# One store of the whole output after the last stage, in place of sixteen stores inside it

## The reference

```python
x = x + attention(layernorm(x))          # 16 heads of 32, causal
x = x + experts(layernorm(x))            # 32 experts, top 8, width 192
x = x + state_space(layernorm(x))        # scan in chunks of 64, inner width 1024
x = x + _L1_ffn_ref(layernorm(x), lut, gate_idx, up_idx, down_idx)

def _L1_ffn_ref(x, lut, gate_idx, up_idx, down_idx):
    gate = _ghost_linear(x, gate_idx, lut)   # x @ lut[gate_idx].T, 512 -> 1376
    up = _ghost_linear(x, up_idx, lut)
    h = jax.nn.silu(gate) * up
    return _ghost_linear(h, down_idx, lut)   # 1376 -> 512
return x
```

## Time and profile before

| | us |
|---|---|
| median of 3 runs | 2704.81 |
| the three runs | 2699.21, 2706.01, 2704.81 |
| the profiled execution, its own time | 2699.21 |
| span of the profile (first to last instruction) | 2697.7 |
| outside the span (2699.21 - 2697.7) | 1.5 |
| TensorE busy in the span | 2395.8 (89%) |
| mean granted clock of TensorE | 0.934 of full speed |

### The profile page before, as it was taken

One profiled execution on the slowest core, in us unless ns is written; L12 is line 12 of the kernel. 1 busy time (PEld: TensorE's weight loads), 2 busy tenths in 40 slices (PEclk: granted clock), 3 DMA queues, 4 the chain that ended last, 5 costly groups with the idle time before them and its releaser, 6 DMA issues. The chain is left out here.

```text
span 2697.7 us, 48584 instructions
## 1 busy us (share of the span) xinstructions
PE 2395.8 (89%) x12839; PEld 1818.7 (67%) x12840; DVE 1580.2 (59%) x3443; ACT 964.2 (36%) x2184; POOL 976.6 (36%) x878
## 2 busy tenths in 40 slices
PE   7969999994756999999999759999979898799998
PEld 5855555552545888888888638888855554688886
DVE  6246566662664455555555466999278786555554
ACT  3114555552153444444444322222255453222221
POOL 3138888885003566666666301111111110000000
PEclk9978999997866999999999979999989999799999
DMA  5469999995345899999988544447499550100001
GB/s 175 124 198 316 346 338 354 335 332 140 84 156 159 243 265 275 236 255 259 275 234 210 89 138 140 172 164 226 136 237 201 132 150 9 40 24 23 23 9 63
DMA packets 263501, 491.18 MB, mean 182 GB/s; under 512 B 32081, under 2 KB 149329, under 8 KB 253650
## 3 DMA queue, kind: packets, MB, share of 16 engines
q1 hardware_dynamic: 197394, 272.17, 33.7%
q0 software_dynamic: 62976, 212.42, 27.9%
q10 hardware_dynamic: 3024, 5.29, 0.6%
HBM read 592.96 MB, written 198.79 MB: 293 GB/s over the span
## 5 line engine op out<-in xcount | busy, mean ns | idle before, releaser
L1367 PE MATMUL m_ps_u<-m_ring,m_xT_hi 128*128 x1280 | 373.0, 353 | 36.7 <-DMA m_ring<-w_split 34.1
L1333 POOL DMA_INDIRECT expert_sum<-x_res,token_of x160 | 254.0, 1587 | 230.1 <-ACT x_res L1435 134.8
L1367 PEld LDWEIGHTS m_ps_u<-m_ring,m_xT_hi 128*128 128x128 f32 x1280 | 238.4, 191 | 40.8 <-issue 40.6
L779 ACT ACTIVATE probs<-ps_c 128x512 f32<-128x512 f32 (+3 forms) x384 | 182.2, 490 | 213.3 <-PE ps_c L712 132.6
L809 DVE TENSOR_REDUCE neg_max<-ps_r 128x1 f32<-128x512 f32 (+3 forms) x256 | 147.6, 589 | 159.3 <-PE ps_r L679 109.6
L1490 DVE SCALAR_TENSOR_TENSOR m_h<-m_silu,m_xg,m_ps_u 128x128 f32<-128x128 f32 x160 | 55.6, 348 | 278.0 <-ACT m_silu L1429 278.0
L1367 PE MATMUL m_ps_u<-m_ring,m_xT_lo 128*128 x640 | 218.3, 341 | 0.0
L1326 POOL DMA_INDIRECT m_xg<-x_rows,token_of x160 | 176.7, 1105 | 103.8 <-issue 99.2
L679 PE MATMUL ps_r<-k_st,q_st 96*128 96x512 f32 (+3 forms) x384 | 163.3, 432 | 46.3 <-DVEq L802 18.2
L1803 PE MATMUL s_ps<-s_x_lo,s_w_hi 128*128 128x512 f32 x512 | 201.2, 393 | 0.0
L1803 PE MATMUL s_ps<-s_x_hi,s_w_lo 128*128 128x512 f32 x512 | 201.0, 393 | 0.0
(11 more groups left out here) (337 smaller groups left out, 5754.4 us busy)
## 6 DMA issues: line engine op xcount, KB each, us to landing
m_ring<-w_split SPq DMA_DIRECT2D x160, 1536.0 KB
m_ring<-w_split SPq DMA_DIRECT2D x160, 768.0 KB
w_split<-e_gu_parts POOLq DMA_DIRECT2D x32, 1536.0 KB
proj<-s_out SPq DMA_DIRECT2D x32, 1024.0 KB, 4.0
e_raw_gu<-w_experts POOLq DMA_DIRECT2D x32, 768.0 KB
w_split<-e_dn_parts POOLq DMA_DIRECT2D x32, 768.0 KB
e_raw_dn<-w_experts POOLq DMA_DIRECT2D x32, 512.0 KB
q_st<-q_parts SPq DMA_DIRECT2D x32, 256.0 KB, 6.3
```

Of the source, the lines that this page charges most:

```text
L779: nc.scalar.activation(probs[a][j % RING][:, :width], ps_c[a][:, :width], ACT.Exp, scale=SCALE).then_inc(exp_done, 1)
L1333: pool.indirect_dma_start(acc[j % 2], rows_at(j), y[j % TURNS], None, bounds_check=PADDED - 1, oob_is_err=True, compute_op=ALU.add).then_i ...
L1367: last = nc.tensor.matmul(ps_u[b % 2][:, :W_UP], x[b % 2][:, k, :], ring[:, first + k * GU_ROW:][:, bass.ds(place, W_UP)], start=(n == 0), ...
```

## The change

The sixteen waits and stores and the final wait leave SP's list in `lut_feed_forward`, which no longer takes `out`. A new function `store_tokens` runs after it, in a block of its own: SP issues one DMA of the whole of `x_res`, 4096 KB, and waits for it. The order of rows in DRAM is the same: each piece is a row of 512 values, 2 KB.

```diff
+def store_tokens(nc, x_res, out):
+    with ExitStack() as ctx:
+        stored = ctx.enter_context(nc.semaphore("out_stored"))
+        block = ctx.enter_context(nc.Block())
+
+        @block.sync
+        def _(sp):
+            sp.dma_start(out.rearrange("(n p) d -> p n d", p=P), x_res[:, :, :]).then_inc(stored, 16)
+            sp.wait_ge(stored, 16)
 
-def lut_feed_forward(nc, x_res, ident, w_ffn, out):
+def lut_feed_forward(nc, x_res, ident, w_ffn):
...
-        stored = sem("out_stored")
...
             load(2 * BODIES, 0, LAST_ROWS)
-            out_rows = out.rearrange("(n p) d -> p n d", p=P)
-            for i in range(TILES):
-                sp.wait_ge(added, SUB + BODIES * RUNS * SUB + i + 1)
-                sp.dma_start(out_rows[:, i, :], x_res[:, i, :]).then_inc(stored, 16)
-            sp.wait_ge(stored, 16 * TILES)
...
-        lut_feed_forward(nc, x_res, ident, w_ffn, out)
+        lut_feed_forward(nc, x_res, ident, w_ffn)
+        store_tokens(nc, x_res, out)
```

## The result

| | before | after |
|---|---|---|
| median of this comparison, us (6 runs each) | 2701.5 | 2722.24 |
| range, us | 2694.64 to 2706.01 | 2717.35 to 2724.44 |
| span of the profiled execution, us | 2697.7 | 2722.9 |
| ratio, with 95% interval | | 1.0067 [1.0048, 1.0086] |

The change makes the kernel slower, by 18 us by this ratio (0.0067 x 2701.5). The ratio is estimated from the executions of one comparison and is not the quotient of the two medians, which lie 20.7 us apart. Three more executions of the changed kernel, outside the six of the table, took 2711.59, 2715.37 and, profiled, 2724.37 us. The forecast was the right way, +10.4 us, but the median of 2722.2 lies above the forecast's range, which ended at 2720. The question is where 18 us come from when one late transfer was priced at 10.4.

What follows compares the result with a forecast made beforehand. Bound by TensorE almost without a gap, then VectorE's last additions and the last store's landing. Terms: -2.2 (last landing) + 0.3 (boundary) + 12.4 (new landing) = +10.4 on 2704.8, giving 2715.2 us; range 2708.4 to 2720.

Steps and rivals of the forecast that it cites:

- Removed stores cost nothing: Last stage: SP's sixteen waits and issues, 0.33 us each, are covered; only the last store's 2.2 us landing is saved.
- rival 3: Last run: store traffic slows matmuls and clock, removal gives 3.2 us back, +7.2 us, within 0.3%; chance 0.03.
- The boundary: Between last stage and new store: ending one block and starting another costs 0.27 us, upper bound 1.03.
- Rival 2: Kernel end: store lands after 13.1 us and block hand-over costs 1.03 us, +11.9 us, 2716.7; chance 0.15.
- The landing: Kernel end: the lone 4096 KB store lands 12.4 us after issue, bounds 11.1 and 13.1.
- twin: In `route`: an existing 4096 KB copy of the same tile in 2 KB pieces, landing after 13.1 us, used as model.
- rival 1: Kernel end: the late store runs at 437 GB/s and lands after 11.1 us, +9.2 us, 2714.0; chance 0.10.
- The deduction of 0.7 us from the twin: In `route`: 272 KB issued ahead on the same queue take 0.7 us of the copy's 13.1, leaving 12.4.
- Rival 4: Last stage: each of sixteen small stores holds up the path 2.2 us; one large store saves 22.5 us, 2682.3; chance 0.01.
- the scatter: Whole executions: three runs before spread from 5.6 us below their median to 1.2 above; two more us added on top.
- as before, at about 2695: End of last stage: sign that the last additions would end at about 2695 us of the span, unmoved.
- a shift of this kind: Whole program: a shift between two programs' medians, unrelated to the tail and as large as run scatter, would refute the forecast.

Runs made afterwards that it cites:

- empty block: Kernel before with its sixteen stores in place, plus one more block at the end where SP only raises a semaphore and waits for it; ratio 1.0002.
- one tile late: Changed kernel, but fifteen tiles are stored in the last stage and only the last, 256 KB, in the new block; ratio 1.0001.
- four tiles late: Changed kernel, but twelve tiles are stored in the last stage and the last four in the new block as one 1024 KB store; ratio 1.0016.
- one store, old block: Kernel before, blocks and semaphores kept, its sixteen stores made one 4096 KB store behind the last addition; ratio 1.0049.
- sixteen late stores: Changed kernel, but the new block issues sixteen 256 KB stores one behind another instead of one of 4096 KB; ratio 1.0027.
- store made twice: Changed kernel with its 4096 KB store issued a second time after the first has landed; ratio 1.0127.
- small chain: Changed kernel plus, behind its store, 23 more 256 KB stores of the first tile, each after the previous landing; ratio 1.0197.
- store made five times: Changed kernel with its 4096 KB store issued five times, each behind the landing of the one before; ratio 1.0185.
- copy of before: The kernel before with nothing edited, compared against itself; ratio 1.0000.

## Why the prediction was right, and where it was not

All runs side by side. The tail's growth is against 2.7 us. The growth of the time is given in two ways, as the ratio's excess times the median of before in the same comparison, and as the difference of the two medians.

| kernel | tail, us | its growth | growth by the ratio | by the medians |
|---|---|---|---|---|
| empty block | 3.2 | +0.4 | +0.5 | -1.5 |
| one tile late | 4.5 | +1.7 | +0.3 | -1.0 |
| four tiles late | 5.0 | +2.2 | +4.3 | +5.3 |
| one store, old block | 13.15 | +10.4 | +13.2 | +8.6 |
| sixteen late stores | 13.0 | +10.3 | +7.3 | +6.7 |
| changed kernel, three times | 13.4 | +10.7 | +18.1, +13.5, +7.6 | +20.7, +10.4, +9.2 |
| store made twice | 26.1 | +23.3 | +34.3 | +30.0 |
| small chain | 59.9 | +57.2 | +53.3 | +54.9 |
| store made five times | 64.0 | +61.3 | +50.0 | +50.1 |

In the nine comparisons whose kernel has the new function, growth by the ratio less growth of the tail lies between -11.3 and +11.0 us, and its mean is +0.1. The late bytes account for the mean growth, and there is no sign of a further cost that all of these programs share.

**Removed stores cost nothing: right.** Sixteen issues and waits went and nothing upstream of the last landing gained. The additions of the last run start a certain time after those of the sixth run before it: 51.2 us before (2641.26 to 2692.48), 51.3 in the copy of before and 51.3 after (2655.74 to 2707.03). The 0.04 us on each set of matmuls, which rival 3 would have given back, are there without any store, as the chain of after shows:

```profile
2672.12 2.76 PE f_ps_g L2401 x12
2674.89 2.77 PE f_ps_u L2401 x12
```

The rest of rival 3, that the stores' traffic pulls down the clock of the last down product, is refuted by three stretches of after, which answer to the earlier trace rows:

```profile
2688.50:2696.90 8.40, 8.40 (x37) 5.97 (x35) 3.77 (x6) 1.21 (x2) 0.00 (x0) 1.00 0.00 0
2697.00:2701.50 4.50, 0.00 (x0) 0.00 (x0) 3.77 (x6) 0.62 (x1) 0.00 (x0) 1.00 0.00 0
2701.50:2707.00 5.50, 5.49 (x12) 3.79 (x12) 0.00 (x0) 0.00 (x0) 0.00 (x0) 0.50 0.00 0
```

No byte moves in any of them, and the granted clock of the last is 0.50 all the same, the lower of its two levels (1.2 of 2.4 GHz), with 5.50 us for the twelve matmuls. What went ahead of it is TensorE idle for 4.5 us.

**The boundary: right.** 0.27 us forecast, 0.28 measured, and 0.25 as the difference between the tails of the two kernels with one late store. Rival 2's 1.03 us did not come.

**The landing: 12.4 forecast, 12.7 measured.** This term was undersized by 0.3 us. These are the landings of the late store and, in the same execution, of the copy in `route`, from the DMA issues of after, as in the earlier trace rows:

```profile
out<-x_res SPq DMA_DIRECT2D x1, 4096.0 KB, 12.7
```

```profile
expert_sum<-x_res SPq DMA_DIRECT2D x1, 4096.0 KB, 13.1
```

The value lies between the twin's 13.1 and the 12.4 that both workings gave. The rate of 385 GB/s held in the slices above, so rival 1's 437 did not come; at that rate the bytes take 10.9 us, and 1.8 of the 12.7 are left as the fixed part where the prediction had 1.5, taken from the 256 KB stores. The deduction of 0.7 us from the twin was too large by the same 0.3. With 12.7 the sum is 12.7 + 0.28 - 2.2 = +10.8, and the tails say +10.7. The page "DMA: Bandwidth & Descriptors" of the Trainium skill (section "Anatomy of one DMA") gives about 2.0 us plus bytes at 436 GB/s, and it gives this fit for DMAs issued from GpSimd, which the prediction did not say; an estimate by it is 11.6 us for this landing. The store issued from SP took 12.7, and the measurement decides.

**Rival 4, faster by batching: refuted.** Sixteen stores in the stage leave a tail of 2.7 us and not sixteen landings. Sixteen late stores and one late store have tails of 13.0 and 13.4 us; the large one saves nothing even where both are late.

**The step that failed is the scatter.** The prediction took the upper side of the scatter from three runs (1.2 us above their median, "two more" added) and expected the additions to end "as before, at about 2695". They ended at 2709.5. The step took one draw for a property of the kernel. The prediction had named a shift of this kind, as large as the scatter and unrelated to the tail, among the signs that would make it wrong, but gave it 2 us of range. Two later medians of the changed kernel, 2717.3 and 2713.6, lie inside the range and the first does not; with this scatter, either is luck. Executions of the kernel before alone span 34 us on one chip (2692.33 to 2726.5), and the comparisons of the changed kernel gave 18.1, 13.5 and 7.6 us, mean 13.1, around a tail that grew by 10.7 each time, which alone is a ratio of 1.0039. The first interval, [1.0048, 1.0086], leaves that value out, and so do the intervals of the store made twice (tail 1.0086) and made five times (1.0227), one on each side. That is three of twelve comparisons, so an interval of one comparison is too narrow here if the tail is the whole cost; only over the table do growth of tail and growth of time agree.

**Where a long attention stage comes from.** In the thirteen profiles the stage lay between 417.1 and 430.1 us, and the five above 424 (the first two of the changed kernel, one tile late, sixteen late, store made twice) have one thing in common that the other eight have not. The rows are from the timelines of VectorE, GpSimd and TensorE near the stage's end, of before and then of after:

```profile
612.67 0.17 DVE L822 TENSOR_TENSOR max_cols<-neg_max,max_cols 128x8 fp32r<-128x8 f32 x1
615.69 4.54 POOL L613 TENSOR_TENSOR wo_lo<-raw_wo,wo_hi 128x2048 fp32r<-128x2048 f32 x1 [0.18 <-POOL wo_hi L610]
```

```profile
619.13 1.89 POOL L621 CAST wo_hi<-raw_wo 128x2048 fp32r<-128x2048 f32 x1
621.20 4.49 POOL L624 TENSOR_TENSOR wo_lo<-raw_wo,wo_hi 128x2048 fp32r<-128x2048 f32 x1 [0.18 <-POOL wo_hi L621]
621.28 4.44 DVE L833 TENSOR_TENSOR max_cols<-neg_max,max_cols 128x8 fp32r<-128x8 f32 x1
625.78 1.62 PE L711 MATMUL ps_turned<-ident_r,max_cols 128*128 128x128 f32 x8 [4.44 <-DVE max_cols L833]
```

VectorE's last subtraction into `max_cols`, of 128 x 8 values, takes 0.17 us before. After, it starts 0.08 us behind GpSimd's subtraction into `wo_lo`, takes 4.44 us and ends 0.03 us behind it. The same 0.08, 4.44 or 4.45 and 0.03 us stand in all five long profiles; in the eight others VectorE's subtraction starts 0.12 to 4.5 us before GpSimd's and takes at most 1.22. TensorE, which needs the result, stands idle for 4.1 to 4.8 us in the five, and behind that in after its granted clock is 0.50 for two stretches of 5 us (columns as in the earlier trace rows):

```profile
621.37:626.37 5.00, 0.59 (x5) 0.59 (x5) 4.95 (x2) 0.64 (x2) 4.32 (x1) 0.98 0.03 11
626.37:631.37 5.00, 5.00 (x18) 2.13 (x17) 0.00 (x0) 1.83 (x4) 0.00 (x0) 0.50 0.25 59
631.37:636.37 5.00, 4.72 (x18) 2.41 (x16) 0.69 (x1) 2.08 (x5) 0.00 (x0) 0.50 0.00 0
```

From the fourth last to the last copy into `y_st` it is 42.1 us in after and 33.5 in before, 40.1 to 43.0 in the five and 33.2 to 34.7 in the eight. So 8.6 of the 11.7 us between the two attention stages arise there, and they go with which of the two engines comes first. This is read from traces; no run moved either instruction.

**What stays open.** Why GpSimd is ahead in one execution and behind in another. None of the four profiles without the new store function has the long form and five of the nine with it have; chance is not excluded as a reading of that, and neither is a cause that depends on the program and acts in some executions only. What is excluded is one that lengthens the stage in every execution: the changed kernel had 418.1 us in its third profile. Attention is not all of the scatter either. From the last copy to the end of the last additions it is 2053.5 to 2066.0 us in the thirteen profiles, and what moves that was not looked into. No version faster than the kernel before came out of the runs: what is left of its tail is one landing of 2.2 us and 0.5 us to the end of the span.

## What to carry to other kernels

In this kernel a store that lay behind the last computation cost its full landing, and stores that lay beside computation cost nothing that the trace shows: at the end of a kernel, store each piece as it is finished, and count only the bytes that can start after the last addition (here 256 KB and 2.2 us, or 4 MB and 12.7). Splitting those late bytes into sixteen stores changed the tail by 0.4 us; how many were late changed it by ten. And where the effect is a few tenths of a per cent, read it in the profile as an interval between two events around the change, not as a difference of spans: here the tails agreed to a tenth of a microsecond while whole executions lay up to 34 us apart.

## What the runs showed of the hardware

Issuing took longer behind other stores. The median issue of a 256 KB store took 0.64 us in the kernel with sixteen late stores, where the same issue took 0.33 before, with each store issued as its tile was finished. As an estimate, 262,144 bytes at 385 GB/s are 0.68 us, so SP was held to about the pace of the data; that this is the reason was not tried:

```profile
L87 SPq DMA_DIRECT2D out<-x_res x16: 365/640/657, 2711.5 to 2720.9; - x16
DMA to landing us min/median/max: 2.0/3.0/3.1
```

The issue of 4.67 us behind the twin points the same way. It cost nothing, as SP had nothing else to do.

A short VectorE operation can last as long as a GpSimd operation that began just ahead of it: 4.44 us against 0.17 for the 128 x 8 subtraction, in five of thirteen profiles.
